# Thirteen context rows to a partition on 123 partitions, in place of twelve on 128 and a remainder of 65

## What is computed

```python
def _L0_xattn_ref(query_input, key_input, value_input, Wq, bq, Wk, bk, Wv, bv):
    q = query_input @ Wq + bq
    k = key_input @ Wk + bk
    v = value_input @ Wv + bv
    attn = jnp.einsum('bqd,bkd->bqk', q, k) / scale
    attn = jax.nn.softmax(attn, axis=-1)
    return jnp.einsum('bqk,bkd->bqd', attn, v)
# x = x + _L0_xattn_ref(_layernorm(x), ctx_1024, ctx_1024, ...)
```

## Time and profile before

| what | value |
|---|---|
| median of three runs | 681.31 us (680.92 to 681.85) |
| the profiled execution | 680.74 us |
| its span, first to last instruction | 679.0 us |
| mean granted TensorE clock | 0.992 |
| packets, bytes | 31,182, 86.47 MB |

### The profile page before, as it was taken

How to read it: one execution, slowest core, us unless ns; L and a number is a source line. 1 busy time by engine, 2 the same in 40 slices (tenths; PEclk the granted TensorE clock), 3 DMA queues, 4 the chain that set the end, 5 groups by cost and what they waited for, 6 DMA issues and landing times. The chain is left out here.

```text
span 679.0 us, 11613 instructions
## 1 busy us (share of the span) xinstructions
PE 611.5 (90%) x4390; PEld 458.7 (68%) x4390; DVE 477.6 (70%) x811; ACT 364.5 (54%) x677; POOL 223.1 (33%) x180
## 2 busy tenths in 40 slices
PE   4999998898997777877878999999999999999997
PEld 3455554464335766776767888887787777889897
DVE  3733343347858989999999736678987778876554
ACT  1311111124559898999999643433566456556342
POOL 2000000000004999999989110033553020331000
PEclk9999999999999899999999999999999979999999
DMA  8999999995620222332321000000100022220000
GB/s 315 398 394 389 390 392 390 395 319 170 141 97 31 95 95 94 116 103 96 123 93 63 1 1 1 16 1 17 35 3 3 1 63 77 51 60 1 32 1 31
DMA packets 31182, 86.47 MB, mean 127 GB/s; under 512 B 8012, under 2 KB 19688, under 8 KB 28952
## 3 DMA queue, kind: packets, MB, share of 16 engines
q1 hardware_dynamic: 30984, 85.67, 35.4%
q10 hardware_dynamic: 144, 0.06, 0.1%
HBM read 83.50 MB, written 1.11 MB: 125 GB/s over the span
## 5 line engine op out<-in xcount | busy, mean ns | idle before, releaser
L732 POOL TENSOR_TENSOR dbu<-du,bs 128x1024 f32<-128x1024 f32 x63 | 148.6, 2397 | 206.7 <-DVE du L924 203.9
L946 DVE TENSOR_TENSOR_SCAN w_in<-hS,dbu 128x1024 f32<-128x1024 f32 x42 | 94.8, 2275 | 0.1
L824 ACT ACTIVATE weighed<-T,CT 128x256 f32<-128x256 f32 x220 | 91.2, 543 | 4.3 <-PE T L1028 3.9
L813 ACT ACTIVATE hS<-delta,negA 128x504 f32<-128x504 f32 x128 | 87.3, 757 | 6.7 <-DVE xn L946 4.2
L1042 PE MATMUL Y<-ident,weighed 128*128 128x128 f32 x512 | 67.7, 275 | 0.1
L1028 PE MATMUL T<-ident,w_in 128*128 128x128 f32 x336 | 46.5, 280 | 23.1 <-ACT weighed L824 14.2
L1042 PEld LDWEIGHTS Y<-ident,weighed 128*128 128x128 f32 x512 | 58.7, 142 | 0.8 <-DVE sres L967 0.3
L1028 PEld LDWEIGHTS T<-ident,w_in 128*128 128x128 f32 x336 | 36.2, 141 | 34.0 <-DVE w_in L946 30.4
L946 DVE TENSOR_TENSOR_SCAN xn<-hS,dbu 128x1024 f32<-128x1024 f32 x22 | 50.1, 2279 | 4.8 <-issue 3.3
L297 PE MATMUL O<-cN,pT 128*64 128x256 f32 x384 | 46.7, 385 | 5.0 <-DMA cN<-in_ctx 4.9
L283 PE MATMUL S<-cT,qkT 128*64 128x512 f32 (+1 forms) x256 | 44.8, 502 | 0.8 <-ACT qkT L383 0.8
(11 more groups left out here) (426 smaller groups left out, 1332.8 us busy)
## 6 DMA issues: line engine op xcount, KB each, us to landing
cT<-in_ctxT SPq DMA_DIRECT2D x8, 3202.0 KB, 22.2
cN<-in_ctx SPq DMA_DIRECT2D x8, 3072.0 KB, 23.9
bs<-b_rows SPq DMA_DIRECT2D x32, 512.0 KB, 3.7
raw_w<-in_w SPq DMA_DIRECT2D x16, 256.0 KB, 2.8
w<-in_w SPq DMA_DIRECT2D x7, 256.0 KB, 7.8
vs<-vx SPq DMA_DIRECT2D x8, 136.0 KB, 2.4
x<-in_x SPq DMA_DIRECT2D x2, 512.0 KB, 5.4
cR<-in_ctx SPq DMA_DIRECT2D x8, 128.0 KB
```

Source lines behind the costliest of these rows:

```text
L732: e.tensor_tensor(dbu[s % NB][:, :, :], half(m.du, s // DS), row, ALU.mult).then_inc(s_bu, 1)
L813: i = e.activation(by_batch(A[s % 2][:, j * HALF:(j + 1) * HALF]), by_batch(m.delta[:, c, h * HALF:(h + 1) * HALF]), ACT.Exp, scale=m.negA ...
L824: i = e.activation(weighed[s % 2][:, q * Q:(q + 1) * Q], T[:, q * Q:(q + 1) * Q], ACT.Copy, scale=c_of(s, q))
L946: e.tensor_tensor_scan(S[s % NS], A[s % 2][:, :], dbu[s % NB][:, :, :].rearrange("p c n -> p (c n)"), 0.0, ALU.mult, ALU.add).then_inc(s_h, 1)
```

## The change

The constants become 13 rows to a partition on 123 full partitions, with a remainder of 2 keys. The large transfer of rows fills partitions 0 to 122 with 13 keys each, one contiguous run of 13,312 bytes a batch. The last two keys (1599 and 1600) go to partition 123 of the same buffer, chunks 0 and 1, in one small transfer on the same semaphore. The buffer cR, its semaphore, its two transfers and the wait ahead of group 3 go. The wait for cN counts both transfers, so 32 in place of 16 a tile. The chunks stay 13: chunks 0 and 1 have 124 keys, the others 123, and the stride of the keys in prob is 13. Nothing else changes.

```diff
-ROWS = LK // P
-MAIN = ROWS * P
-REST = LK - MAIN
+ROWS = LK // P + 1
+FULL = LK // ROWS
+REST = LK - FULL * ROWS
 def load_rows(e, k, i, r):
-    e.dma_start(k.cN[r][:, :, :, :], k.ctx[2 * i:2 * i + 2, 0:MAIN, :].rearrange("b (p c) d -> p b c d", c=ROWS)
+    e.dma_start(k.cN[r][0:FULL, :, :, :],
+                k.ctx[2 * i:2 * i + 2, 0:FULL * ROWS, :].rearrange("b (p c) d -> p b c d", c=ROWS)
                 ).then_inc(k.s_dN[r], 16)
 def load_rest(e, k, i, r):
-    for rows in (slice(0, 64), slice(64, REST)):
-        e.dma_start(k.cR[r][rows, :, :], k.ctx[2 * i:2 * i + 2, MAIN + rows.start:MAIN + rows.stop, :].rearrange("b p d -> p b d")
-                    ).then_inc(k.s_dR[r], 16)
+    e.dma_start(k.cN[r][FULL:FULL + 1, :, 0:REST, :], k.ctx[2 * i:2 * i + 2, FULL * ROWS:LK, :].unsqueeze(0)
+                ).then_inc(k.s_dN[r], 16)
...
         def keys(c):
-            return slice(c, c + (P - 1) * ROWS + 1, ROWS) if c < ROWS else slice(MAIN, LK)
+            return slice(c, c + (n_keys(c) - 1) * ROWS + 1, ROWS)
         def n_keys(c):
-            return P if c < ROWS else REST
+            return FULL + 1 if c < REST else FULL
...
-                if g == 3:
-                    e.wait_ge(k.s_dR[r], 32 * (i // 2 + 1))
                 for c in groups[g]:
                     for b in range(2):
-                        v = cN[r][:, b, c, :] if c < ROWS else cR[r][:, b, :]
-                        j = e.matmul(O[64 * b:64 * b + 64, 0:D], pT[0:n_keys(c), c, 64 * b:64 * b + 64], v,
-                                     start=c == 0, stop=c == ROWS)
+                        j = e.matmul(O[64 * b:64 * b + 64, 0:D], pT[0:n_keys(c), c, 64 * b:64 * b + 64],
+                                     cN[r][0:n_keys(c), b, c, :], start=c == 0, stop=c == ROWS - 1)
...
-                    e.wait_ge(s_dN[(i - 1) % 2], 16 * ((i - 1) // 2 + 1))
+                    e.wait_ge(s_dN[(i - 1) % 2], 32 * ((i - 1) // 2 + 1))
```

More of the change, by code:

```diff
@@ L135, in cross_attention @@
         qbk = sb("qbk", [P, TILES])
-        cT, cN, cR, s_dT, s_dN = k.cT, k.cN, k.cR, k.s_dT, k.s_dN
+        cT, cN, s_dT, s_dN = k.cT, k.cN, k.s_dT, k.s_dN
         prob = [sb(f"prob{r}", [P, LK]) for r in range(2)]
-        pT = sb("pT", [P, ROWS + 1, P])
+        pT = sb("pT", [P, ROWS, P])
         mx = sb("mx", [P, 1])
@@ L3005, in perceiver @@
         k.cN = [sb1(f"cN{r}", [P, 2, ROWS, D]) for r in range(2)]
-        k.cR = [sb1(f"cR{r}", [REST, 2, D]) for r in range(2)]
-        k.s_dR = [sem(f"a_dR{r}") for r in range(2)]
         k.w_v0 = t["wv0"]
```

## The result

The changed kernel takes 985.91 us (median of four, 984.85 to 986.97) against 681.12 us for the one before: ratio 1.448, interval 1.445 to 1.451. The forecast was 933 us with a range up to 980, so the result lies outside it. The direction and the three engines held; of the 305 us the forecast had 252.

A forecast was written before the change was run, and what follows sets the result against it. The first stage (cross attention) was taken as balanced, TensorE and transfers close to level. 680.74 us plus 248.2 (shift) plus 3.5 (clock) gave 932.4; with the median 0.6 above the profiled execution, 933 us, range 915 to 980.

The forecast's parts named there:

- The equal split over three engines: Large context-row load, outermost count 123: three engines carry it, 41 partitions each, where sixteen carried 8 each.
- Rivals A: Large load: sixteen engines after all, with unequal shares; time 680 to 682.5 us, 676 at best; chance 0.08.
- B: Large load: two of three engines stand idle up to 14.5 us a load; +116, 1049 us; chance 0.04.
- C: Large load: one engine alone carries it, 121.7 us each; 1582 us; chance 0.02.
- Step 2: Three engines' queues: loads follow one another with a 7.6 us share of cT between (8.5 at lower rate), never running dry.
- Step 1: Large load on three engines: 26.9 GB/s each, 40.6 us a load (45.1 at 24.2), for 7.3 us before.
- My upper bound (24.2 GB/s for each engine): Large loads at the crowded stretches' rate: last landed at 436.4 us; with 8 us of clock, 978 us.
- Steps 3: Start of the first large load: after 8.32 MB ahead of it, at 23.9 us, as now.
- 5: Start of values(7): waits for the last load alone, at 394.9 us for 146.7, a shift of +248.2 us.
- 6: From values(7) to the scan layer: 9.6 us now; w_in, queued behind the last load, needs 2.4 us and stays hidden.
- Step 7: TensorE's clock after long waits: a stretch at its lower level, lengthening the last tile by 0 to 8 us, taken 3.5.
- Step 8: Removed cR transfers and waits, added small transfer, chunk shapes, stride 13 (nothing): sum -1 to +1 us, hidden, taken 0.

The follow-up runs named there:

- e3: The kernel before, twelve rows to a partition kept, with its large load cut at partition 123 (123 and 5 partitions): 977.3 us, ratio 1.435.
- e4: The changed kernel without the column (transposed context) loads of tiles 2 to 7; output not the reference's: 892.96 us.
- e6: The changed kernel with one more wait on SyncE, holding back a tile's columns until the rows of two tiles earlier have landed: 954.2 us, ratio 1.401.
- e13: The kernel before, with the rest of each batch loaded as 128 consecutive rows on 128 partitions, 65 of them used: 676.2 us, ratio 0.992.
- e10: The changed kernel's 13-row layout with loads of 128 partitions, one per batch, and no transfer for a rest: 686.3 us, ratio 1.0078 to the kernel before.
- e8: The kernel before, with the 65 remaining rows loaded only for tiles 0 and 1; output not the reference's: 676.4 us, ratio 0.992.
- e7: Transfers alone, no computation, over different partition ranges and pairs: 425 GB/s for 128 partitions, 210 for two halves of 64; no kernel time given.
- e9: Transfers alone: columns beside one engine writing its own or foreign partitions, rows beside two engines; 426 GB/s beside one in its own group.
- e11: Transfers alone: columns beside two engines writing own, foreign or mixed partition groups, long or 2 KB runs; 301 GB/s with both in one foreign group.
- e12: The kernel before, each chunk given its own key stride and number of keys; output not the reference's; costly transposes took 373 to 391 ns, no kernel time given.

## Why the prediction went wrong where it did

**The equal split over three engines: right.** The packets of q1 are 29,648 as worked out, the share with rows alone is 0.19, and e3 carries it over to the old layout. Rivals A, B and C fall. Step 2 holds too: the three engines never run dry (e4).

**Step 1, a load alone: right.** 40.6 us forecast, 40.9 to 41 measured (e4).

**Step 1, "with three engines at work nothing is crowded": this is the step that failed.** It took the rate from a stretch in which, as I now read it, every engine wrote its own group of partitions. The changed load gives each engine 41 partitions, most of them in groups of others, and as long as the next tile's columns move beside it, both go at half rate (216 GB/s at a share of 1.01). (That the 41 lie side by side is inferred: neighbours written together would be slow, and the load alone is not.) The fifteen-odd us of overlap a tile cost about 8. In all: without columns values(7) starts at 355.6 us (e4), with six shares of 7.6 it would be 401; it started at 449.8. So 49 of the 55 us are the overlap, and 6 are the rate, the landings and the weights behind the last load. e6 takes the overlap away and gets 33 back, net of 2 us a tile for its own wait. My upper bound (24.2 GB/s for each engine) was the rate of a stretch that was itself mildly disturbed by the rest (387 GB/s, 416 in e13); it is no bound for two streams that collide. The nearest row was not near.

**Steps 3, 5 and 6: right.** The first load starts where it did, the stage alone is shifted, w_in is hidden. One reading ahead of them was loose: the 16 to 17 us that a tile was said to cost TensorE held its waits for rows; without them a tile costs 15.06 us.

**Step 7, the clock: right in kind.** It was granted at 0.50, the 1.2 GHz level, once TensorE had stood idle between tiles, as the rows at 46 to 50 and 168 to 188 us show. From values(7) to the scan layer it is 12.0 us for 9.6: +2.4. Of it 1.7 are the first sixteen matmuls (3.68 for 1.95 us), which is the clock, where I took 3.5; the other 0.7 are the transposes of step 8.

**Step 8, the transposes at nothing: wrong, and hidden.** They cost 1.3 us more a tile (e10). The stride, which I named, is indeed nothing; what I did not look at is that a chunk of 123 keys in place of 128 is also another shape for the transpose, and an odd one (410 ns for 290). In the changed kernel they lie beside the wait for rows and cost almost nothing. With the transfers mended they decide the sign: e10 is 5.4 us slower than the kernel before. The matmul with 123 rows for 65 was costed rightly.

**Step 8, the rest: its size was missed.** I put its removal between -1 and +1 us, from its bytes and issues; e8 measured 4.8.

## What to carry to other kernels

Read the outermost count of a transfer before its bytes: in every transfer counted here the engines took equal whole shares of it, and a count like 123 leaves three of sixteen at work. Then ask which partitions the engines write at the same time: a load of all 128 ran at 425 GB/s, another range beside it can halve both, and a small remainder was cheaper here as a padded 128-partition load than as a snug one (5.5 us). And an edit that trims a few keys off a chunk is not free on TensorE because the work shrinks: compare the transposes shape by shape, since 124 keys and 123 keys were 275 and 410 ns.

## What was not expected of the hardware

- Two engines that write two foreign groups of partitions bring sixteen from about 425 to 203 to 218 GB/s; one such engine leaves 390 to 400, and two in one foreign group 301 (e7, e9, e11). The cause of the spread to engines that share no group with them is open.
- A load of 64 partitions moves 210 GB/s with all sixteen engines busy, one of 120 moves 201, one of 112 moves 256, one of 128 moves 425 (e7).
- A transpose of fp32 columns takes 275 ns with 124 columns at a stride of 13 and 410 ns with 123 at the same stride (e10); with 119 to 122 columns at strides of 8 to 11 the odd numbers take 373 to 384 ns and the even ones 273 (e12). The reason is open.
